# A wait for the last chunk's landing ahead of each group's first chunk, in the scatter passes of a four-layer graph network

## What is computed

```
# layer 2 (row = src, col = dst)
msg = norm[:, None] * x[col]
agg = segment_sum(msg, row)                 # by source
out = relu(agg @ W.T + b)
# layer 3
gate = silu(edge_attr @ W1.T + b1) @ W2.T + b2 + adapt_logit
msg  = gate * h[dst] * (cw * mj)[:, None]
agg  = segment_sum(msg, src) / clip(segment_sum(mj, src))   # by source
x    = layernorm(h + agg) * gamma + beta
```

## Time and profile before

| | |
|---|---|
| median of 3 runs | 20233.9 us |
| profiled execution | 20236.5 us, span 20234.7 us |
| pass 2, scatter loop | 9432 to 14665 us of the span |
| tail of pass 2 and epilogue 2 | 14665 to 14943 us |
| pass 3, scatter loop | 14943 to 19968 us |
| tail of pass 3 and epilogue 3 | 19968 us to the end |
| GpSimd busy over the span | 55% |
| TensorE busy, weight loads | 56%, 47% |
| VectorE busy | 48% |
| ScalarE busy | 19% |

### The profile page before, as it was taken

One profiled execution on the slowest core, in us unless ns is written; L12 is line 12 of the kernel. 1 busy time (PEld: TensorE's weight loads), 2 busy tenths in 40 slices (PEclk: granted clock), 3 DMA queues, 4 the chain that ended last, 5 costly groups with the idle time before them and its releaser, 6 DMA issues. The chain is left out here.

```text
span 20234.7 us, 302760 instructions
## 1 busy us (share of the span) xinstructions
PE 11419.2 (56%) x63600; PEld 9543.6 (47%) x63601; DVE 9780.5 (48%) x26342; ACT 3891.4 (19%) x10412; POOL 11133.6 (55%) x11410
## 2 busy tenths in 40 slices
PE   6666666666656666665666545554464334555545
PEld 5555555555534444343444444444453224444445
DVE  3555555555566666664111455555442225555556
ACT  1000000000122122222333111111122222333331
POOL 4555555555544454444555556666635666666663
PEclk9999999999966666665555555555555555555555
DMA  4333333333211111112333222222222222222222
GB/s 110 77 76 76 76 76 77 77 77 77 67 40 38 39 41 42 41 41 64 90 91 90 78 69 69 70 70 68 64 70 82 77 80 73 75 76 76 76 75 52
DMA packets 1574947, 1407.00 MB, mean 70 GB/s; under 512 B 982792, under 2 KB 1441691, under 8 KB 1570446
## 3 DMA queue, kind: packets, MB, share of 16 engines
q1 hardware_dynamic: 597320, 636.63, 12.3%
q0 software_dynamic: 410000, 462.80, 9.7%
q10 hardware_dynamic: 567508, 306.27, 5.6%
HBM read 984.46 MB, written 420.15 MB: 69 GB/s over the span
## 5 line engine op out<-in xcount | busy, mean ns | idle before, releaser
L1752 POOL DMA_INDIRECT order<-l_msg,l_uring x6250 | 6081.7, 973 | 4212.9 <-DMA order<-l_msg,l_uring 2071.4
L1895 PE MATMUL ps<-l_ordb,l_ohs 128*128 128x49 f32 x15040 | 3307.2, 414 | 2680.7 <-DVE acc L1795 1365.9
L1895 PEld LDWEIGHTS ps<-l_ordb,l_ohs 128*128 128x128 f32 x15040 | 3240.4, 332 | 2747.3 <-DVE acc L1795 1406.5
L548 POOL DMA_INDIRECT l_rows<-btab,l_sd x3125 | 3024.2, 968 | 2368.4 <-DMA l_rows<-btab,l_sd 1388.8
L1088 POOL DMA_INDIRECT l_rows<-y,l_sd x1875 | 1822.2, 972 | 1960.5 <-DMA l_sd<-in_sd 907.1
L1795 DVE TENSOR_TENSOR acc<-acc,ps 128x49 f32 x7520 | 1526.0, 206 | 2158.8 <-issue 1031.0
L689 PE MATMUL ps<-l_rhs,l_lhs 64*128 x6250 | 1455.8, 426 | 824.5 <-DVE l_rows L625 506.5
L689 PEld LDWEIGHTS ps<-l_rhs,l_lhs 64*128 64x128 f32 x6250 | 1358.7, 327 | 911.7 <-issue 910.2
L704 PE MATMUL ps<-l_ohe,l_hid 128*128 128x32 f32 x6250 | 1384.7, 402 | 606.4 <-ACT l_hid L734 606.4
L704 PEld LDWEIGHTS ps<-l_ohe,l_hid 128*128 128x128 f32 x6250 | 1351.8, 331 | 656.7 <-ACT l_hid L734 622.6
L1929 PE MATMUL ps<-l_win,l_oht 96*128 x6250 | 533.1, 241 | 1901.5 <-DVE l_oht L1817 876.6
(11 more groups left out here) (313 smaller groups left out, 14535.0 us busy)
## 6 DMA issues: line engine op xcount, KB each, us to landing
l_ordb<-order SPq DMA_DIRECT2D x752, 250.0 KB
l_dstb<-ids SPq DMA_DIRECT2D x250, 600.0 KB
order<-l_msg,l_uring POOLq DMA_INDIRECT x6250
order<-l_zero ACTq DMA_DIRECT2D x125, 775.0 KB
l_eat<-in_ea40P SPq DMA_DIRECT2D x625, 120.0 KB
gates<-l_made ACTq DMA_DIRECT2D x625, 120.0 KB
l_gin<-gates SPq DMA_DIRECT2D x125, 600.0 KB
l_rows<-btab,l_sd POOLq DMA_INDIRECT x3125
```

The source lines that it names most:

```text
L548: pool.indirect_dma_start(rows[:, t, :], None, d["btab"], bass.IndirectOffsetOnAxis(ap=sd[:, t, 0:1], axis=0)).then_inc(gat[c], 16)
L1752: pool.indirect_dma_start(d["order"], bass.IndirectOffsetOnAxis(ap=uring[:, t:t + 1], axis=0), msg[:, t, :], None).then_inc(sc[c], 16)
L1895: done = t.matmul(red[b % 2][:, k * MW:(k + 1) * MW], ohs[b][:, k, :], ordb[b][:, k, 0:MW], start=True, stop=True)
```

## The change

GpSimd now also waits ahead of chunk 0 of a group, in all groups but the first of a pass, until chunk 4 of the group before has landed. As the wait's value would be zero in group 0, that group gets a loop of its own with one round.

```diff
-            with pool.Fori(0, NG) as g:
+
+            def scatter(g, rested):
                 for c in range(NCH):
                     pool.wait_ge(u_ready, g * NCH + c + 1)
                     if gated:
...
                     if c:
                         pool.wait_ge(sc[c - 1], (g + 1) * 16 * CT)
                         pool.nop(nofuse=True)
+                    elif rested:
+                        pool.wait_ge(sc[NCH - 1], g * (16 * CT))
+                        pool.nop(nofuse=True)
                     for t in range(c * CT, (c + 1) * CT):
                         pool.indirect_dma_start(d["order"], bass.IndirectOffsetOnAxis(ap=uring[:, t:t + 1], axis=0),
                                                 msg[:, t, :], None).then_inc(sc[c], 16)
+
+            with pool.Fori(0, 1) as g:
+                scatter(g, False)
+            with pool.Fori(1, NG) as g:
+                scatter(g, True)
```

## The result

| | before | after |
|---|---|---|
| median | 20242.6 us (4 runs, 20230.3 to 20262.2) | 20477.4 us (4 runs, 20467.1 to 20484.3) |
| profiled execution | 20236.5 us, span 20234.7 us | 20484.3 us, span 20482.4 us |

The ratio is 1.0115, with a 95% interval of 1.0097 to 1.0132. The kernel is slower, as forecast, by 235 us where 312 were forecast.

What follows compares the result with a forecast made beforehand. GpSimd's scatters and waits for their landings were taken to bound groups 40 to 124 of passes 2 and 3. 158 + 151 - 15 + 18 = 312 us on the median of 20233.9 gave 20546 us, range 20488 to 20638.

Steps and rivals of the forecast that it cites:

- What one wait costs, 1.86 and 1.78 us: Time one wait adds ahead of chunk 0: 1.86 us in pass 2, 1.78 in pass 3, at least 1.68.
- Groups 40 to 124: 85 groups a pass, where GpSimd sets the pace: the wait adds 158 us in pass 2, 151 in pass 3.
- the tenth of a us: Sign of a wrong forecast: gaps of chunks 1 to 4 change by more than this in the mean.
- Rival 1: The other waits shrink: all 680 gaps fall to the floor of 1.98 us, 190 us come back, time 20356; 5%.
- Count the wait at nothing at these 8 places: Groups 68, 88, 103 and 115 of each pass: chunk 1's gap shrinks as chunk 0 starts later, -15 us.
- Pass 2, groups 1 to 39: the wait costs nothing: GpSimd waits there for ScalarE ahead of chunk 1, 6.8 us above the floor, which covers the wait: 0 us.
- Pass 3, groups 1 to 9: nothing: GpSimd waits there for VectorE ahead of chunk 0; both waits run side by side: 0 us.
- Pass 3, groups 10 to 39: 0.6 us a group: SP's chain runs at the same pace and absorbs most of the wait: 18 us, between 0 and 50.
- chunk 3 falls below 3.2: Sign in pass 3's groups 10 to 39: the gap ahead of chunk 3, 3.23 us before, shrinks below 3.2.
- The rest: 0: Group 0's own loop, its branch and code, and the waits' own instructions are hidden: 0 us.
- Rival 2: Groups 40 to 124: the look-up chain needs more than 41.7 us a group, so time stays at 20234; 3%.
- what it gains the kernel gains: Claim for groups 40 to 124 of both passes: GpSimd sets the pace, its losses and gains are the kernel's.

Runs made afterwards that it cites:

- p2_head: The kernel before with the wait ahead of chunk 0 only in pass 2's groups 1 to 39: 20098.5 us, ratio 0.9935 on chip 11.
- no_wait2: The kernel before without the wait ahead of chunk 2 in groups 40 to 124 of both passes: 20376.4 us, ratio 1.0080 on chip 10.
- gin_small_none: The kernel before with pass 3's gates load cut to one tile in place of 25: 19831.4 us, ratio 0.9978 on chip 13.
- The pause: The kernel before with a GpSimd memset ahead of chunk 0 in pass 2's groups 1 to 39: ratio 0.9926 on chip 10, 1.0029 on chip 13.

## Why the prediction was right or wrong

**What one wait costs, 1.86 and 1.78 us: right.** The gap ahead of chunk 0 in groups 40 to 124 went from 0.30 and 0.31 to 2.00 and 2.03, that is 1.70 and 1.72 added, at the lower end (1.68) of the bounds. (The shortest gaps of the trace are 1.94 and not 1.98; 1.98 is the usual one.)

**"Groups 40 to 124": wrong, by the other four gaps.** The prediction let them stay, but for a new phase worth some 20 us. In pass 2 those of chunks 2 and 4 fell from 2.34 to 1.98 and 2.03: with the 0.02 of chunk 3, -0.7 us a group. In pass 3 chunk 4's rose by 1.16, and chunk 2's fell by 0.13. So the terms of 158 - 7 and 151 - 7 us became 76 and 224. The other four gaps changed by -0.17 and +0.25 us each in the mean, over the tenth of a us that the prediction had named as the sign of being wrong. The failing step was to price one gap and to take the loads' place beside the other four as given. For pass 3 the trace after shows the gates load in the last us before the landing of chunk 3; for pass 2 it is read from the gaps alone which ones fell, and why was not tried. Rival 1 named the first half, gaps that fall to the floor. The rule that it quoted from the Trainium skill, "DMA: Bandwidth & Descriptors", section "Latency and other measured facts" (a lighter load makes the fixed cost smaller), goes with this much of the trace: 1.98 is the floor before and after, and a landing beside SP's large loads takes 2.4 to 4. But not all gaps came down, as the rival had it: what changed is which landing meets a load.

**"Count the wait at nothing at these 8 places", -15 us: wrong in size.** Where SP reads four pieces at once, chunk 1's gap fell from 4.67 to 4.40 at group 88, at the four places of pass 2 from 4.84 to 4.30 in the mean, in pass 3 from 4.80 to 4.10. That is 5 us in all. I had assumed that the load's end sets the gap.

**"Pass 2, groups 1 to 39: the wait costs nothing": wrong, -162 us.** It was true that GpSimd had 6.8 us to spare ahead of chunk 1 in the mean. The failing step was to take ScalarE's lateness as ScalarE's own pace, which the wait can't touch. I didn't follow the wait one engine further: ScalarE waited 482 us for TensorE, and TensorE's own counts of its look-up came up to 10.7 us late beside GpSimd's run of ten. GpSimd was waiting for a consequence of its own unbroken run, on the chips that show this. A sum of terms with a floor at zero can't find a gain of this kind; the prediction gave 1% to faster, and a version that is 0.65% faster (p2_head) was inside the change.

**"Pass 3, groups 1 to 9: nothing": right**, -6 us.

**"Pass 3, groups 10 to 39: 0.6 us a group": wrong, 3.5.** The cover that I saw in SP's chain (40.9 us a group) was none, as the chain moved with GpSimd. ScalarE, who waits for the gates before, waits for scatters after (pass 3, about groups 11 to 38; before, then after):

```profile
ACT l_under L1971 <- DMA l_gin<-gates: 352.4, 28, 13.8
```

```profile
ACT l_msg L2029 <- DMA order<-l_msg,l_uring: 816.9, 134, 8.9
```

And the delays that I expected to fade, "chunk 3 falls below 3.2", did fade (1.98) but came back at two places, chunk 0 with 3.12 and chunk 4 with 3.42. The gaps add up to 9.92 us before and 12.90 after. The remaining 0.5 us are scatters that take longer beside the others' work, 1.327 from start to start against 1.299.

**"The rest: 0"**: right within 3 us.

**Rival 2** (another chain needs over 41.7 us and hides the wait) fell. no_wait2 shows its true half: going faster than some 39 to 40 us a group, GpSimd meets the other chain. The margin is on the other side of the change. My sentence "what it gains the kernel gains" is refuted by that run.

**How near the number was is luck.** The terms of the five stretches were off by -75, +80, +86, -162 and -6 us. With 12 us outside of them that comes to -65: 248 us between the spans, where the terms give 313. On chip 13, where pass 2's groups 1 to 39 have nothing to give back, the wait costs 547 us (measured with the small gates load).

## What to carry to other kernels

An engine that waits for another may wait for an effect of its own behaviour: follow the chain of waits until it ends at work, or at a stop that nothing in the profile explains, before calling it cover. When loads and scatters run at the same pace, a wait that is added or removed shifts their phase, and every landing has to be priced anew by the load that it now meets; a few hundredths of a us for "the other gaps" was far too small a bound where one of them grew by 1.16. And a wait of one price had four different worths in four stretches here, so the best version with it has it only in pass 2's groups 1 to 39 (p2_head, 0.9935; a memset in its place did as well, 0.9926), and even that depends on the chip.

## What the runs showed of the hardware that was not expected

- On chips 10 and 11 (and in the two traces of the result) the counts of TensorE's look-up come late while GpSimd issues ten indirect DMAs without a break: the last one 7.1 us in the mean and up to 10.7 before, 1.8 in the mean and up to 3.9 after, where the run is five. The step behind them begins 0.02 to 0.03 us after the last count. VectorE's and ScalarE's counts are not late (0.01 us). A memset of 1.70 us between the scatters helps as well as a wait for a landing. Whether the matmuls run late or only their counts, and how the one engine holds the other, was not shown; no row names it.
- In pass 3's groups 40 to 124 of the kernel before, sequencer instructions of VectorE, ScalarE and SP that wait for nothing take over 0.5 us in 180, 208 and 343 cases, most of them some 0.7. On chip 13 (gin_small_none) none of them takes over 0.25.
- On chip 13 the same code has no such stop (39.60 us a group against 44.5 to 47.1), and the kernel before takes 19874 us there against 20235 and 20244. The pause is -0.7% on the one and +0.3% on the other.
- The landing of a chunk of five scatters of 25.6 KB each is seen 1.94 to 1.98 us behind its last descriptor at the earliest, in every kernel run. Beside four pieces of `order` it is 3.7 to 5.3 (groups 68, 88, 103 and 115). With SP's load of the gates sent off in the last us before it, it is 3.8 in the mean (51 landings, pass 3's groups 40 to 124 after), and 2.0 to 2.3 with the load over 3 us earlier.
